# Keys and queries laid out in row halves, and one step of maxima behind the mix of every tile

## The chip, the cores and the metric

One core of a Trainium2 chip runs the whole program. The metric is device time in microseconds (us), from the launch to the end on that core; the number given for a kernel is the median of several runs.

## The reference

Two blocks, each a cross attention and a mixture of experts, on x of shape (32, 56, 256): 32 batches of 56 tokens, 256 features. The attention is the part that the change touches:

```python
q_big  = einsum('bshk,hkq->bshq', layernorm(x) @ Wq.T, w_kc_q)      # 16 heads, 192 wide; layer 0 applies rope
kv     = rope(ctx)                                                    # ctx: (32, 1500, 64)
q_r    = einsum('bshq,hqr->bhsr', q_big, W_qr)
k_r    = einsum('bld,hdr->bhlr', kv, W_kr)
attn   = softmax(einsum('bhsr,bhlr->bhsl', q_r, k_r))                 # over 1500 keys
ctx_c  = einsum('bhsl,bld->bhsd', attn, kv)
x      = x + (ctx_c through w_kc_kv) @ Wo.T
```

After it come, in layer 0, a router over 16 experts of which 4 are taken and a shared expert, and in layer 1 a dense feed-forward with eight low-rank adapters, two of them for each token.

## The kernel before, in words

The weights are merged once at the start (W_kr into the queries' side), so that every head's query is 64 wide and meets the same 64-wide keys. Then each layer runs a loop over 4 groups of 8 batches; a group has 448 tokens, and a batch has 16 heads x 56 tokens = 896 query columns.

A group begins with the queries of all heads (`qwide`, `query`). To keep precision, a value is split in a part that the fast matmul form holds exactly and a rest: `kparts` has the keys' high part in rows 0 to 63 and their low part in rows 64 to 127; `qhigh` holds the high part of the queries twice, once in each half of the rows; `qlow` holds the low part in rows 0 to 63 and, in row 64, the shift of the softmax (minus the maximum). `kones` has the high keys again and a row of ones.

Then comes the attention loop over the batches j, and in it over 12 tiles t of 125 keys:

- `score` (L863, L866): four matmuls, two for each half of the 896 columns, into one of two double banks (`wide`). ScalarE takes the exponential into `prob` (L1098, four buffers).
- `mix` of the tile before (L880): prob x values, the two halves of the columns into partitions 0 to 63 and 64 to 127 of one bank.
- the sums of `prob`: GpSimd adds tiles 0 to 9 (L1211), VectorE tiles 10 and 11 (L1345), and then merges the two (L1351).
- `smax` (L841): matmuls of 128 query rows with 500 keys for the maxima of the next batch, seven rows x three column blocks = 21 a batch. VectorE reduces each to one column (L1324). They turn over the last three of four `single` banks; `SMAX_PACE` puts three of them behind the scores of tiles 2 to 8 and none at tiles 0, 1, 9, 10 and 11.
- `maxneg`, `maxT`: the maxima are joined, transposed and moved by a DMA into the shift row.
- `norm` and `share`: the sums over the partitions (L887), their reciprocal in two halves (L1370, at tiles 1 and 9) and the product with the mixed values (L1375, at tile 11).
- in layer 0 the rope of batch j + 2 (L1255 and L1262 on VectorE at tile 10, L1186 and L1187 on GpSimd) and the transposes of the keys of batch j + 1 (L806, with a copy on ScalarE, L1065, and a subtraction on VectorE, L1292) at tile 0; a DMA stores keys and values. Layer 1 fetches them (L721, L722, L729).

`schedule` writes this order out as one list of steps. Every engine walks the whole list and takes what is its own, strictly in this order, and waits on semaphores. `Regions` counts the uses of each bank: `room` makes TensorE wait until the bank's last content is drained, and what stands behind the waiting matmul in TensorE's list waits too. SP's queue, which issues all DMAs, walks the same list.

## Time and profile before

| what | value |
|---|---|
| median of 3 runs | 3490.61 us (3485.57 to 3497.17) |
| the profiled execution | 3502.88 us, its span 3501.1 us |
| TensorE (PE) matmuls busy | 3137.0 us, 90% |
| VectorE (DVE) busy | 2264.2 us, 65% |
| GpSimd (POOL) busy | 1689.7 us, 48% |
| ScalarE (ACT) busy | 1349.1 us, 39% |
| TensorE clock granted, mean | 0.938 |
| a group of layer 0, of layer 1 | some 454 us, some 388 us |

Matmuls are pipelined and their ends are modelled, so the durations of TensorE's records overlap: its real prices are the distances between the starts of blocks. The granted clock is 1.0 at 2.4 GHz and 0.5 at 1.2 GHz. An fp32 matmul is written as two records; one on split values (fp32r) is one record. "Idle before" a row names what ended the wait.

### The profile page before, as it was taken

What the parts mean: (1) busy time and instruction counts of PE and PEld (TensorE: products, weight loads), DVE (VectorE), ACT (ScalarE), POOL (GpSimd) and SP (SyncE); (2) the same over time, 40 slices, a digit from 0 to 9 for tenths busy, and PEclk for the clock granted to TensorE, in tenths of its full rate; (3) what the DMA queues carried; (4) which work ended last, traced back from release to release, by engine and by line L of the source; (5) the groups of instructions that cost most, each with busy time, mean ns of one, the idle gap of its engine ahead of it and who ended that gap; (6) DMA issues with size and microseconds to landing.
All of it is one profiled execution on the core that took longest, in us unless ns stands there. A gap on an engine that the chain in (4) does not pass through costs nothing. (4 is left out here: it accounts for less than half of the span.)

```text
span 3501.1 us, 38073 instructions
## 1 busy us (share of the span) xinstructions
PE 3137.0 (90%) x12936; PEld 1862.8 (53%) x12936; DVE 2264.2 (65%) x3034; ACT 1349.1 (39%) x1939; POOL 1689.7 (48%) x984
## 2 busy tenths in 40 slices
PE   7699978999789998899988699879998799779997
PEld 6455456555465554655547455455545455454545
DVE  3578756788567885578856467546755477555755
ACT  3235533354342553425434244333433344333442
POOL 0467624676236762367733266315642366215641
PEclk9899989999899999899999799989998899899998
DMA  7411013111131110221102211111110211111110
GB/s 258 132 39 54 32 52 96 53 40 45 36 99 48 54 49 28 81 74 42 50 35 59 93 54 40 50 54 58 53 50 6 77 53 42 47 57 55 54 53 6
DMA packets 95735, 206.20 MB, mean 59 GB/s; under 512 B 9967, under 2 KB 58783, under 8 KB 94134
## 3 DMA queue, kind: packets, MB, share of 16 engines
q1 hardware_dynamic: 95542, 203.61, 17.9%
q8 instruction: 123, 2.02, 0.2%
q14 instruction: 70, 0.57, 0.1%
HBM read 153.44 MB, written 49.91 MB: 58 GB/s over the span
## 5 line engine op out<-in xcount | busy, mean ns | idle before, releaser
L1211 POOL TENSOR_TENSOR sum_pool<-sum_pool,prob 125x896 f32<-125x896 f32 x472 | 996.6, 2111 | 232.9 <-ACT prob L1098 229.3
L1098 ACT ACTIVATE prob<-wide 125x896 f32<-125x896 f32 x768 | 704.8, 918 | 949.1 <-PE wide L866 945.1
L1324 DVE TENSOR_REDUCE maxpart<-single 128x1 f32<-128x500 f32 x1344 | 823.8, 668 | 282.6 <-PE single L841 282.1
L880 PE MATMUL single<-prob,kv 125*64 125x448 f32 x3072 | 752.1, 568 | 0.8
L863 PE MATMUL wide<-qhigh,kparts 128*125 128x448 f32 x1536 | 523.4, 422 | 10.2 <-DMA kones<-keys_merged 10.2
L863 PEld LDWEIGHTS wide<-qhigh,kparts 128*125 128x125 f32 x1536 | 231.3, 189 | 504.8 <-issue 503.4
L866 PE MATMUL wide<-qlow,kones 65*125 65x448 f32 x1536 | 445.6, 372 | 0.0
L841 PE MATMUL single<-kparts,qhigh 128*128 128x500 f32 x1344 | 406.4, 409 | 17.0 <-DVE kparts L1292 5.9
L1211 POOL TENSOR_TENSOR sum_pool<-prob 125x896 f32<-125x896 f32 x64 | 134.8, 2105 | 392.5 <-ACT prob L1098 392.5
L866 PEld LDWEIGHTS wide<-qlow,kones 65*125 65x125 f32 x1536 | 292.2, 190 | 29.8
L841 PEld LDWEIGHTS single<-kparts,qhigh 128*128 128x128 f32 x1344 | 257.5, 193 | 80.6 <-issue 26.1
L880 PEld LDWEIGHTS single<-prob,kv 125*64 125x64 f32 x3072 | 152.5, 135 | 256.1 <-issue 247.9
L1164 POOL TENSOR_TENSOR wexp_low<-wexp_low_values,wexp_high 128x768 fp32r<-128x768 f32 x68 | 128.6, 1894 | 243.5 <-ACT wexp_high L1035 243.5
L1370 DVE RECIPROCAL recip<-total 128x224 f32<-128x224 f32 x112 | 173.4, 1548 | 111.9 <-ACT total L1111 111.9
L1159 POOL TENSOR_TENSOR w_low<-w_low_values,w_high 128x384 fp32r<-128x384 f32 (+1 forms) x128 | 112.1, 879 | 186.8 <-ACT w_high L1023 186.8
L777 PE MATMUL wide<-x_high,w_high 128*96 128x448 f32 (+1 forms) x344 | 144.5, 420 | 64.3 <-POOL w_low L1159 64.2
L1196 POOL TENSOR_TENSOR sum_pool<-prob 96x448 f32<-96x448 f32 x128 | 152.0, 1206 | 61.1 <-DVE prob L1313 61.1
L1345 DVE TENSOR_TENSOR sum_dve<-prob 125x896 f32<-125x896 f32 x64 | 86.1, 1345 | 142.8 <-ACT prob L1098 142.8
L1218 POOL TENSOR_TENSOR hsum<-hid 128x448 f32<-128x448 f32 (+1 forms) x24 | 27.5, 1147 | 254.8 <-DVE hid L1483 254.8
L1186 POOL TENSOR_TENSOR rope_s<-raw,sink 125x384 f32<-125x384 f32 x32 | 37.0, 1156 | 198.7 <-POOLq L684 119.1
L778 PE MATMUL wide<-x_high,w_low 128*96 128x448 f32 (+1 forms) x344 | 131.3, 382 | 0.0
L779 PE MATMUL wide<-x_low,w_high 128*96 128x448 f32 (+1 forms) x344 | 131.0, 381 | 0.0
(272 smaller groups left out, 4414.1 us busy)
## 6 DMA issues: line engine op xcount, KB each, us to landing
wexp_low_values<-in_experts SPq DMA_DIRECT2D x68, 384.0 KB, 3.1
keys_merged<-kparts SPq DMA_DIRECT2D x32, 750.0 KB, 4.8
kparts<-keys_merged SPq DMA_DIRECT2D x32, 750.0 KB, 4.6
raw<-in_ctx SPq DMA_DIRECT2D x33, 375.0 KB
w_low_values<-w_merged SPq DMA_DIRECT2D x64, 192.0 KB, 2.4
values_merged<-kv SPq DMA_DIRECT2D x32, 375.0 KB
kv<-values_merged SPq DMA_DIRECT2D x32, 375.0 KB
kones<-keys_merged SPq DMA_DIRECT2D x96, 125.0 KB, 2.6
```

Of the source, the lines that this page charges most:

```text
L777: pe.matmul(dst, w_hi, x_hi, start=start, stop=False)
L778: pe.matmul(dst, w_lo, x_hi, start=False, stop=False)
L779: return pe.matmul(dst, w_hi, x_lo, start=False, stop=stop)
L841: pe.matmul(acc[:, 0:LB], qhigh[:, j, t * 128:(t + 1) * 128], kparts[:, kdst(j), b * LB:(b + 1) * LB], start=True, stop=True).then_inc(*R. ...
L863: pe.matmul(acc[0:LP, half, 0:HQ], kparts[:, kdst(j), cols], qhigh[:, j, q], start=True, stop=False)
L866: mm = pe.matmul(acc[0:LP, half, 0:HQ], kones[:, cols], qlow[:, j, q], start=False, stop=True)
L880: mm = pe.matmul(mix_acc[64 * half:64 * half + DC, 0:HQ], kv[:, j % 3, t, :], prob[:, (j * LT + t) % NPROB, half * HQ:(half + 1) * HQ], st ...
L1098: nc.scalar.activation(prob[:, n_ % NPROB, :].rearrange("p (a b) -> p a b", a=2), acc[0:LP, :, 0:HQ], ACT.Exp)\
L1196: nc.gpsimd.tensor_tensor(qr[:, h % 2, half, :], qa[:, h % 2, half, :], qb[:, h % 2, 1 - half, :], ALU.add)\
L1211: nc.gpsimd.tensor_tensor(dst, first_in, prob[:, n_ % NPROB, :], ALU.add).then_inc(s["pool_sum"], 1)
L1324: V.tensor_reduce(maxpart[:, j % 2, t, b:b + 1], acc[:, 0:LB], AX.X, ALU.max).then_inc(*R.signal_drained(kind, *key))
L1370: V.reciprocal(recip[:, cols], sums[:, cols])\
```

## The change

The 64-wide products are laid out in halves of the rows. `qhigh` and `qlow` hold heads 0 to 7 in rows 0 to 63 and heads 8 to 15 in rows 64 to 127, half as many columns as before; the keys, high and low, stand in both halves. A `score` is then four pairs of 64-row matmuls: high x high, low x high, high x low, and a row of ones with the shift. The second copy of the keys comes by DMA (in layer 0 from the first half, in layer 1 each half is fetched). `kones` and its copies go.

A step of maxima is a pair too: 112 query rows of either half with the same 500 keys, into the pair of banks 4 and 5 (`PAIR`), reduced by one instruction over 2 x 500 columns. A batch has 12 such steps instead of 21 matmuls; there is one at each tile, behind the mix, four tiles ahead of its use. `Regions` makes the pair exclude its two banks.

Queries are made in pairs of heads (column halves in layer 0, merged weights of two heads in layer 1). Keys' transposes come one a tile at tiles 5, 6 and 7, two batches ahead, all on bank 3; the rope moves to tile 3. For batches 0 to 6 the reciprocal of the sums is taken on 112 x 8 values: two small DMAs, one reciprocal, a store to DRAM and two broadcast loads replace the two of 128x224.

```diff
-NMAX = NQ // 128
+TQ = HQ // 4
+NMAX = 8
+NPAIR = H // 2
+PAIR = 6
-SMAX_PACE = (0, 0, 3, 3, 3, 3, 3, 3, 3, 0, 0, 0)
-EARLY_MAX = 1
-HSLOTS = (4, 6)
+EARLY_MAX = 4
+HSLOTS = (4, 8)
...
+    def maximum(j, n):
+        add("smax", j, n % 4, n // 4, region=PAIR)
...
         for t in range(LT):
+            ahead = (j + 1, t + EARLY_MAX) if t + EARLY_MAX < LT else (j + 2, t + EARLY_MAX - LT)
             add("score", j, t, region=t % 2)
-            for _ in range(SMAX_PACE[t]):
-                if ahead:
-                    row, c = ahead.pop(0)
-                    add("smax", j + 1, row, c, region=turn())
             if j + 1 < BG and t == 8:
                 add("maxneg", j + 1)
             if last is not None:
                 add("mix", *last)
                 if last[1] == LT - 1:
                     add("context", last[0])
+            if ahead[0] < BG:
+                maximum(*ahead)
             last = (j, t)
-            if layer == 0 and 0 < j < BG - 1 and t == 0:
-                keys(j + 1)
             if t == 1 and j:
-                add("norm", j - 1, region=turn())
-            if t in SHARE_AT and j:
-                add("share", j - 1, SHARE_AT.index(t))
+                add("norm", j - 1, region=3)
+            if layer == 0 and t in (5, 6, 7) and j + 2 < BG:
+                keys(j + 2, t - 5)
+            if t == 3 and j:
+                add("spread", j - 1)
+            if t == SHARE_AT[2] and j:
+                add("share", j - 1, 2)
             if j + 1 < BG and t == 9:
-                add("maxT", j + 1, region=turn())
-            if layer == 0 and t == 10 and j + 2 < BG:
+                add("maxT", j + 1, region=3)
+            if layer == 0 and t == 3 and j + 2 < BG:
                 add("rope", j + 2)
...
+        meets = {PAIR: (PAIR, 4, 5), 4: (4, PAIR), 5: (5, PAIR)}
...
                     elif kind == "smax":
-                        pe.matmul(acc[:, 0:LB], qhigh[:, j, t * 128:(t + 1) * 128], kparts[:, kdst(j), b * LB:(b + 1) * LB],
-                                  start=True, stop=True).then_inc(*R.signal_filled(kind, *key))
+                        for half in range(2):
+                            mm = pe.matmul(acc[0:TQ, half, 0:LB], qhigh[rows_of(half), j, t * TQ:(t + 1) * TQ],
+                                           kparts[rows_of(half), j % 3, 0, b * LB:(b + 1) * LB], start=True, stop=True)
+                        mm.then_inc(*R.signal_filled(kind, *key))
...
                     elif kind == "score":
+                        for i, (part, q) in enumerate(((0, qhigh), (1, qhigh), (0, qlow))):
+                            for half in range(2):
+                                pe.matmul(acc[0:LP, half, 0:HQ], kparts[rows_of(half), j % 3, part, cols], q[rows_of(half), j, :],
+                                          start=(i == 0), stop=False)
+                        if t == 0:
+                            pe.wait_ge(s["shift_loaded"], 32 * (j + 1))
                         for half in range(2):
-                            pe.matmul(acc[0:LP, half, 0:HQ], kparts[:, kdst(j), cols], qhigh[:, j, q], start=True, stop=False)
-                        for half in range(2):
-                            mm = pe.matmul(acc[0:LP, half, 0:HQ], kones[:, cols], qlow[:, j, q], start=False, stop=True)
+                            mm = pe.matmul(acc[0:LP, half, 0:HQ], c["ones_row"][rows_of(half), 0:LP], shift[rows_of(half), j % 2, :],
+                                           start=False, stop=True)
...
-                        V.tensor_reduce(maxpart[:, j % 2, t, b:b + 1], acc[:, 0:LB], AX.X, ALU.max).then_inc(*R.signal_drained(kind, *key))
+                        V.tensor_reduce(maxpart[:, j % 2, t:NMAX:4, b], acc[0:TQ, :, 0:LB], AX.X, ALU.max).then_inc(*R.signal_drained(kind, *key))
```

SP's part of it, in the order of the list:

```diff
                     if kind == "fetch":
-                        sp.dma_start(kparts[:, kdst(j), :].bitcast(F32), scratch["keys"][BG * g + j]).then_inc(s[f"keys_moved_{j % 3}"], 16)
+                        for half in range(2):
+                            sp.dma_start(kparts[rows_of(half), j % 3, :, :].rearrange("p a l -> p (a l)").bitcast(F32),
+                                         scratch["keys"][BG * g + j]).then_inc(s[f"keys_moved_{j % 3}"], 16)
...
+                    if kind == "keyT":
+                        sp.wait_ge(*R.drained("keyT", j, b))
+                        sp.dma_start(kparts[DC:2 * DC, j % 3, :, cols].bitcast(F32), kparts[0:DC, j % 3, :, cols].bitcast(F32))\
+                            .then_inc(s[f"keys_twice_{b}"], 16)
...
+                    if kind == "norm" and key[0] < BG - 1:
+                        sp.wait_ge(*R.drained("norm", j))
+                        for half in range(2):
+                            sp.dma_start(packed[half * ZP:(half + 1) * ZP, :], total[64 * half:64 * half + 1, :]).then_inc(s["sums_packed"], 16)
+                    if kind == "spread":
+                        sp.wait_ge(s["packed_recip"], j + 1)
+                        sp.dma_start(scratch["zrec"][j].rearrange("(p c) -> p c", c=ZC), packed_recip[:]).then_inc(s["recip_stored"], 16)
+                        sp.wait_ge(s["recip_stored"], 16 * (j + 1))
+                        if j:
+                            sp.wait_ge(s["ctx_ready"], j)
+                        for half in range(2):
+                            sp.dma_start(recip[64 * half:64 * half + 64, :],
+                                         scratch["zrec"][j:j + 1, half * HQ:(half + 1) * HQ].broadcast_to([64, HQ])).then_inc(s["recip_spread"], 16)
```

## Rows read from the trace of the kernel before

**Rows 1.** The page, parts 1 and 5: engines, and the sums on GpSimd.

```profile
PE 3137.0 (90%) x12936; PEld 1862.8 (53%) x12936; DVE 2264.2 (65%) x3034; ACT 1349.1 (39%) x1939; POOL 1689.7 (48%) x984
...
L1211 POOL TENSOR_TENSOR sum_pool<-sum_pool,prob 125x896 f32<-125x896 f32 x472 | 996.6, 2111 | 232.9 <-ACT prob L1098 229.3
```

**Rows 2.** Windows: start:end, length, busy us by engine, granted clock, DMA share, GB/s.

```profile
665.30:896.70 231.40, 231.40 (x1018) 118.99 (x1017) 176.14 (x221) 116.36 (x156) 156.24 (x77) 0.99 0.11 39
...
1953.00:1997.70 44.70, 32.74 (x127) 26.97 (x128) 23.84 (x41) 14.35 (x35) 11.69 (x16) 0.81 0.38 115
1997.70:2221.90 224.20, 224.20 (x944) 112.70 (x945) 144.39 (x190) 96.69 (x117) 141.07 (x67) 0.99 0.14 42
```

**Rows 3.** Timeline in a loop of layer 0: start, us, engine, line.

```profile
318.68 0.68 PE L863 MATMUL wide<-qhigh,kparts 128*125 128x448 f32 x2
...
319.60 0.85 PE L841 MATMUL single<-kparts,qhigh 128*128 128x500 f32 x3
...
320.03 1.85 DVE L1324 TENSOR_REDUCE maxpart<-single 128x1 f32<-128x500 f32 x3 [0.75 <-PE single L841]
320.38 0.97 PE L880 MATMUL single<-prob,kv 125*64 125x448 f32 x4
...
321.28 0.67 PE L863 MATMUL wide<-qhigh,kparts 128*125 128x448 f32 x2
...
322.29 0.97 PE L880 MATMUL single<-prob,kv 125*64 125x448 f32 x4
...
327.23 0.62 DVE L1375 TENSOR_TENSOR ctx_n<-ctx_raw,recip 128x448 f32<-128x448 f32 x1
```

**Rows 4.** The chain that ended last, in order of time: four fp32 records, 128 columns wide.

```profile
3480.67 1.50 PE single L990 x4
```

**Rows 5.** Groups on VectorE in a loop of layer 0 (665.3 to 896.7): busy us, mean ns.

```profile
L1324 DVE TENSOR_REDUCE maxpart<-single 128x1 f32<-128x500 f32 x144 | 88.4, 669 | 31.9 <-PE single L841 31.8
L1370 DVE RECIPROCAL recip<-total 128x224 f32<-128x224 f32 x14 | 21.7, 1548 | 7.7 <-ACT total L1111 7.7
L1255 DVE TENSOR_TENSOR rope_c<-raw,cosk 125x768 f32<-125x768 f32 x6 | 15.4, 2559 | 0.0
...
L1351 DVE TENSOR_TENSOR sum_dve<-sum_dve,sum_pool 125x896 f32<-125x896 f32 x7 | 10.4, 1485 | 0.2
L1262 DVE TENSOR_TENSOR kv<-rope_c,rope_s 125x768 f32<-125x768 f32 x6 | 7.5, 1255 | 0.2
```

**Rows 6.** Groups ahead of that loop (572.5 to 665.3), queries of layer 0.

```profile
L1196 POOL TENSOR_TENSOR sum_pool<-prob 96x448 f32<-96x448 f32 x32 | 38.0, 1206 | 15.3 <-DVE prob L1313 15.3
...
L1312 DVE TENSOR_TENSOR prob<-wide,cosq 96x896 f32<-96x896 f32 x16 | 17.4, 1086 | 12.5 <-PE wide L779 11.3 <-POOL sum_pool L1196 1.2
...
L1159 POOL TENSOR_TENSOR w_low<-w_low_values,w_high 128x384 fp32r<-128x384 f32 x16 | 16.0, 1003 | 6.2 <-ACT w_high L1023 6.2
```

**Rows 7.** Groups on VectorE in a loop of layer 1 (1997.7 to 2221.9).

```profile
L1351 DVE TENSOR_TENSOR sum_dve<-sum_dve,sum_pool 125x896 f32<-125x896 f32 x7 | 7.6, 1092 | 0.2
```

**Rows 8.** Timeline at the start of a group of layer 0, GpSimd idle.

```profile
575.64 0.96 DVE L1255 TENSOR_TENSOR rope_c<-raw,cosk 125x768 f32<-125x768 f32 x1 [5.14 <-issue]
```

**Rows 9.** DMA issues of the whole run: count, KB each, median us to landing.

```profile
kparts<-keys_merged SPq DMA_DIRECT2D x32, 750.0 KB, 4.6
...
kones<-keys_merged SPq DMA_DIRECT2D x96, 125.0 KB, 2.6
```

**Rows 10.** Timeline from the last maxima of batch 0 to the loop.

```profile
657.18 0.17 DVE L1331 TENSOR_REDUCE maxneg<-maxpart 128x7 f32<-128x21 f32 x1
...
665.31 0.92 ACT L1098 ACTIVATE prob<-wide 125x896 f32<-125x896 f32 x1 [2.44 <-PE wide L866]
```

**Rows 11.** Timeline of TensorE among the queries of layer 1.

```profile
1971.09 0.44 PE L777 MATMUL wide<-x_high,w_high 128*128 128x448 f32 x1 [4.11 <-POOL w_low L1159]
...
1973.01 0.57 PE L778 MATMUL single<-x_high,w_low 128*128 128x448 f32 x1
1973.38 0.57 PE L779 MATMUL single<-x_low,w_high 128*128 128x448 f32 x1
```

More of the change, by code:

```diff
@@ L47 @@
 MT = -(-HID // 128)
+ZP, ZC = 56, 8
 SHARE_AT = (1, 9, 11)
[L50 removed]
 RT = NT // 112
@@ L133, in schedule @@
+    last_maxima(0)
     add("maxneg", 0)
[L134 removed]
     if layer == 0:
[L137 to L138 removed]
+        keys(1, 0)
+    add("maxT", 0, region=3)
+    if layer == 0:
+        keys(1, 1)
+        keys(1, 2)
+    for n in range(EARLY_MAX):
+        maximum(1, n)
     last = None
[L140 to L141 removed]
     for j in range(BG):
[L144 removed]
```

299 lines of the change are left out of this document (146 added, 153 removed).

## The prediction

> **What bounds the kernel now.** I read the page first: TensorE is busy 90% of the span, VectorE 65%, GpSimd 48% [rows 1]. By stage, the attention loops (eight batches of twelve tiles) take 231.4 us in a group of layer 0 and 224.2 in one of layer 1, and in both TensorE is never idle at a granted clock of 0.99 [rows 2]. Eight such loops are 4 x (231.4 + 224.2) = 1822 us, half the time. VectorE is busy 176 of 231 us in layer 0: second in line. The stretch ahead of the loop, where queries are made, is 44.7 us in layer 1, and TensorE is not full there (busy 32.7, granted 0.81) [rows 2]; in layer 0 it is longer and holds the maxneg and exp of [rows 10] at its end.
>
> Inside a loop the timeline of TensorE gives the price of each step [rows 3]: scores (four matmuls) to mix 1.01 us (321.28 to 322.29), mix to scores 0.90 (320.38 to 321.28), so a tile without maxima is 1.91. With three maxima it is 2.60 (318.68 to 321.28): 0.23 for one. Check: 96 x 1.91 + 144 x 0.23 = 216.5; the other 15 of the 231.4 are seven norms (about a mix each), seven maxT and six runs of key transposes.
>
> **The scores: nothing.** Four matmuls of 128 and 65 rows become four pairs of 64-row halves (three products and the shift). No row of before shows row halves. The nearest is the mix, two 64-column halves: four records in 0.90 us [rows 3], where four records of the same 448 columns on the full array take 1.50 [rows 4]. So halves of columns do run at the same time, and I take halves of rows to do so: four units before, four after. Bounds: no overlap costs four units a tile; imperfect overlap is the 0.15 us by which 0.90 exceeds half of 1.50, over two passes 0.075 a pair.
>
> **The maxima on TensorE: a gain.** 21 matmuls a batch become 12 pairs. In the loops 144 x 0.23 = 33.1 us become 80 x 0.23 = 18.4 (16 of the 96 pairs of a group stand ahead of the loop): -14.7 a loop, -118 over eight. Transposes, norm and maxT now stand between maxima and scores, in halves of columns amid halves of rows, and the transposes in three runs instead of one. A change of form costs about 0.1 us (1.01 for a score block against 4 x 0.23 x 448/500 = 0.82, two changes a tile): +18 (0 to 37).
>
> **The maxima on VectorE: no gain, and one buffer.** A reduction of 128x500 takes 0.669 us and a PSUM read of 896 columns 1.086 [rows 5, 6]: 1.05 ns a column, so the new 1000 columns take 1.19. Twelve of these are 14.3 us a batch, the old 21 were 14.0. What changes is the room. Before, three banks turn and the pace leaves tiles 0, 1, 9, 10 and 11 free of maxima. After, each tile has one step of maxima, and all use the one pair of banks. TensorE waits at a step until the reduction of the step before is over, and behind the waiting matmul stand the next scores, the exponentials and everything else. Count from the start of a step of maxima: the reduction begins after 0.1 (load) + 0.43 (319.60 to 320.03 [rows 3]) and ends at 1.72; other VectorE work W and the next reduction end at 2.91 + W; 0.06 later TensorE may fill the pair for the step after that, and it wants to at 2 x (1.91 + 0.23) = 4.28. So it stalls for W - 1.3, where that is positive. Maxima back to back cost 1.72 + 0.06 = 1.78 each.
>
> - Batch boundary, between the maxima of tiles 11 and 0: ctx_n 0.62, the last sum and the merge of sums, both 896 columns from SBUF at 1.09 [rows 3, 7], are 2.8, a stall of 1.5. Six boundaries a loop, eight loops: +72 (with the mean of layer 0, 1.49 [rows 5], for both, W is 3.6 there: +91).
> - The rope of layer 0, now at tile 3, where GpSimd adds sums in 2.11 us out of 2.14 [rows 1, 5]. Before it began at the end of GpSimd's run. rope_c takes 0.96 us with GpSimd idle [rows 8] and 2.56 on average in the loop, the final add of the same size 1.26 [rows 5], 0.96 if alone. With the small reciprocal (some 0.18, as maxneg [rows 10]): W = 0.18 + 2.56 + 1.26 = 4.0, a stall of 2.7, 24 times: +65. Bounds: GpSimd never in the way, W = 2.1, 24 x 0.8 = 19; both operations held for a whole 2.11, W = 0.18 + 2 x 3.07 = 6.3, 24 x 5.0 = 120.
> - The keys' subtractions (64x500, taken at the 0.67 of a reduction of 500 columns) come one a tile: below 1.3, nothing.
>
> On this the trace shows rope_c at 0.96 alone and 2.56 in the loop [rows 5, 8]. The Trainium skill ("SBUF — State Buffer", on who interferes with whom) says that GpSimd and a VectorE operation with two SBUF inputs take an exclusive lock for the whole instruction. By that rule the second operation could wait too, and the sum would have the 120 in place of the 65, 55 us more; the trace agrees for one operation and leaves open who wins the next turn.
>
> **Reciprocals.** Two of 1.55 us a batch [rows 5] go; they have no place of their own in the stalls above, so this is what keeps those from being worse. In their place come two small moves, one reciprocal, a store and two broadcasts. The sums are copied about 2.0 us after the maxima of tile 1 (norm as a mix 0.9, a copy of half the columns of an exponential 0.5, signals; an estimate), and VectorE comes to the reciprocal at 4.28 + 1.72 = 6.0: cover of 4 us for moves of which the small ones take 2.6 [rows 9]. In layer 1 the fetch of keys and values is issued at tile 0 ahead of them, and it grows from 750 + 375 to 2 x 750 + 375 KB because each row half gets its copy. At 4.6 us for 750 KB [rows 9] that is 11.5 us, where the reciprocal is wanted 9.6 after the maxima of tile 0 (3 x 2.14 + 1.5 + 1.72): at most 1.9 late, W = 2.1, a stall of 0.8. Bounds 0 and 20 x 0.8 = 16; I take +5. SP waits in its own queue for the store of the reciprocals, with the next context load and the key copies behind it; these are wanted tiles later. In layer 0 a 256 KB copy of the keys into the other rows leaves 2.4 us after the maxima of tile 5 and is wanted at tile 8, 4.9 later; it should land between the 2.6 of 125 KB and the 4.6 of 750 [rows 9]. The shift leaves at tile 9 behind the key store of tile 7 (375 + 750 KB) and is wanted some 4 us later. Both nothing; where that cover fails, up to 3 us x 24 = 72.
>
> **Ahead of the loops.** Layer 0: the keys' three transposes share one bank, so TensorE waits twice for a copy and a subtraction of 500 columns, 0.67 each by the reduction, and signals: +3.2. Queries take half the passes, but three maxima in a row now cost 1.78 each, and GpSimd needs 2 x 1.21 + 1.00 = 3.4 us a head [rows 6], where TensorE's part now is 12 x 0.20 + 1.5 = 3.9 [rows 3, 4]: nothing (-8 to +4). At the end a full row of maxima stays after the last query (+2.6), and the first maxima of batch 1 wait for keys transposed, split and copied across (about 5.4 us after maxneg, then four at 1.78 and the scores, 12.8 in all) where today exp follows maxneg by 8.1 us (657.18 to 665.31) [rows 10]: +4.7. Together +10.5 a group, +42 (20 to 70). Layer 1: 48 matmuls of 0.2 us and a 4.11 us wait for weights [rows 11] go, but sixteen maxima at 1.78 (at half clock, where one takes 0.2 more, 1.98) are 28 to 32 us of a chain with little beside it. With 9.6 us of queries (part of them at the lower clock), two waits and the scores, the 44.7 us become 44 to 49: +6 for four groups (-4 to +16). Setup copies less: -5.
>
> **Sum.** -118 + 18 + 72 + 65 + 5 + 42 + 6 - 5 = +85. The profiled run took 3502.88 us (span 3501.1 and 1.8 around it); the median of the runs shown is 3490.61, 0.35% below. Against the median the sum gives 3490.6 + 85 = 3575, with its own range of 3515 to 3640 (down by the rope near its low bound, up by the rope near its high one or the clock, below).
>
> **A price that the sum leaves out.** After 4.1 us of idleness the matmuls soon stood 0.37 us apart (1973.01 to 1973.38) and not 0.20, the lower of the two clocks [rows 11]; if a stall of 2.7 us brings three such microseconds, it adds 1.5 us, 24 x 1.5 = 36. It is in the own range.
>
> **Rivals.**
> - *Vector work stays out of the way* (faster). Place: the two clusters in the loop. If TensorE never waits for the pair, the 137 us of stalls go: 3438, and with shorter stretches ahead of the loops 3400. For it: VectorE has 24 us of work in a batch of 28. Against: the order of its queue puts 2.8 and 4.0 us between two reductions that hold the only buffer. It decides where the 72 stalls cost under (137 - 85) / 72 = 0.7 us on average. Chance 0.26.
> - *Halves overlap only in part.* 0.075 us a pair, four pairs a tile and 768 tiles (+230), less the 0.20 x 768 = 154 of change of form that the block already holds, and 0.075 x 768 = 58 for maxima: +134, 3709. Chance 0.12. In numbers of a page: the Trainium skill ("TensorE: Matmul & The Clock Gate", Part 3, measured speedup) has four row tiles at 3.07 times one; an estimate from it is 1.3 units a pair, 0.06 us over, (4 + 1) x 768 x 0.06 = 230, and 3805. No run here shows row tiles yet.
> - *Halves do not overlap.* 4 x 0.205 x 768 = +630, maxima 0.23 x 768 = +177, stalls 75 less (tiles 1.04 us longer, 72 places): 4307. For it, only that nothing in the trace shows row halves; against it, the mix. Chance 0.07.
> - *It nets out*: the rope and the stretches ahead of the loops at their low bounds, -118 + 18 + 72 + 19 + 20 - 4 - 5 = +2, 3492. Chance 0.08.
>
> **Chances and range.** The forecast has 0.47. A measurement here can tell about 0.3% (10 us) from no change. Slower: 0.47 + 0.12 + 0.07 = 0.66; same 0.08; faster 0.26. The range runs from 3405, into the faster case, to 3690; left out are the bottom of that case, most of the part overlap and no overlap, about 0.2.
>
> **What would show it.** Right: score block near 1.0 us and a tile at 2.14 in quiet steps; TensorE idle before the maxima of tiles 1 and 5, released by the reduction, 1.5 and 2.7 us; reductions of 1.19; a loop of layer 0 near 245 us and of layer 1 near 220. Wrong: no idle time at those maxima (faster), a score block of 1.3 or more (part overlap) or 1.8 (none), or idle time ahead of the reciprocal released by a move.

## The result, and the profile after

Before 3488.1 us (3482.3 to 3497.2), after 3787.9 us (3783.9 to 3792.3), medians of four runs each. The ratio on record is 1.0846, 95% interval 1.0825 to 1.0867 (the two medians alone give 1.0860). The change costs 300 us. The forecast was 3575 with a range from 3405 to 3690: the sign was right, the size short by 213 us, and the time lies 98 us above the range. The profiled execution has a span of 3783.0 us, 282 more than before.

The exponentials on ScalarE cut the span (the time from the first instruction to the last) into stages: a loop is counted from the start of its first exponential to the start of its last. All numbers are us; the last column is the last experiment, in which all mends stand together:

| stretch | before | after | difference | forecast | last experiment |
|---|---|---|---|---|---|
| start to the first loop | 209.3 | 233.4 | +24 | | 221.3 |
| four loops of layer 0 | 922.7 | 1079.4 | +157 | +51 | 906.6 |
| between them | 668.5 | 716.0 | +48 | | 682.4 |
| from layer 0 to layer 1 | 197.2 | 205.7 | +9 | | 194.7 |
| four loops of layer 1 | 896.4 | 911.7 | +15 | -9 | 846.7 |
| between them | 491.6 | 520.0 | +28 | | 481.5 |
| the end | 115.4 | 116.6 | +1 | | 116.7 |
| all outside the loops | 1682.0 | 1791.7 | +110 | +43 | 1696.6 |

The forecast's column is its sum split by layer: for a layer (-118 + 18 + 72) / 2 = -14, with 65 for the rope in layer 0 and 5 for the reciprocals in layer 1.

The page of after, part 1 and the rows of part 5 that answer to [rows 1, 5] (us busy, mean ns; idle time before, and who ended it):

```profile
PE 3122.5 (83%) x16008; PEld 1727.9 (46%) x16008; DVE 2096.5 (55%) x2343; ACT 1261.1 (33%) x1747; POOL 1654.5 (44%) x952
...
L1317 DVE TENSOR_REDUCE maxpart<-pair 112x2 f32<-112x1000 f32 x768 | 920.4, 1198 | 739.8 <-PE pair L840 739.8
...
L840 PE MATMUL pair<-kparts,qhigh 64*112 64x500 f32 x1536 | 403.4, 522 | 286.5 <-DVE maxpart L1317 264.1
```

TensorE is busy as long as before (3122 for 3137 us) in a longer span, and VectorE does less (2097 for 2264 us). 264 us of TensorE's idleness stand in front of the pair of banks. The windows of a loop of layer 0, of the stretch ahead of a loop of layer 1, and of that loop, as in [rows 2]:

```profile
741.60:1012.00 270.40, 242.42 (x1414) 113.04 (x1414) 157.76 (x150) 107.25 (x135) 156.59 (x77) 0.93 0.24 57
2180.00:2234.60 54.60, 28.97 (x92) 19.10 (x94) 24.20 (x25) 8.28 (x19) 5.75 (x8) 0.63 0.55 125
2234.60:2465.00 230.40, 214.22 (x1344) 100.51 (x1343) 122.19 (x121) 97.34 (x117) 140.59 (x67) 0.98 0.21 50
```

Before, the granted clock was 0.99 in both loops and 0.81 in the stretch ahead of one [rows 2]; now it is 0.93, 0.98 and 0.63. So idleness is one part of the cost and a lower clock the other.

**The rope in layer 0.** Timeline of a batch, from the reciprocal of tile 3 on (start, us, engine; in brackets the idle time ahead):

```profile
353.03 0.19 DVE L1350 RECIPROCAL packed_recip<-packed 112x8 f32<-112x8 f32 x1
353.14 1.49 DVE L1248 TENSOR_TENSOR rope_c<-raw,cosk 125x768 f32<-125x768 f32 x1
...
353.96 2.62 POOL L1204 TENSOR_TENSOR sums<-sums,prob 125x896 f32<-125x896 f32 x1
...
354.67 2.73 DVE L1255 TENSOR_TENSOR kv<-rope_c,rope_s 125x768 f32<-125x768 f32 x1
...
357.32 1.19 DVE L1317 TENSOR_REDUCE maxpart<-pair 112x2 f32<-112x1000 f32 x1
...
358.56 0.55 PE L840 MATMUL pair<-kparts,qhigh 64*112 64x500 f32 x2 [2.81 <-DVE maxpart L1317]
```

Between the end of the reduction ahead (353.11, from 351.91) and the next one at 357.32 lie 4.2 us of other work; TensorE waits 2.81 at the maxima of tile 5. The forecast had 4.0 and 2.7. What it left beside the sum stands in the windows behind that wait:

```profile
355.70:358.50 2.80, 0.05 (x2) 0.00 (x0) 2.80 (x2) 0.10 (x1) 2.66 (x2) 1.00 0.26 82
358.50:362.90 4.40, 4.34 (x19) 2.14 (x19) 1.88 (x3) 1.50 (x2) 0.83 (x1) 0.61 0.30 98
362.90:367.00 4.10, 4.10 (x28) 2.18 (x28) 2.52 (x3) 1.65 (x3) 3.12 (x2) 1.00 0.35 77
```

After 2.8 us without a matmul TensorE works the next 4.4 us at a granted clock of 0.61, mostly the lower level, 1.2 GHz.

**The shift in layer 0.** SP's queue and TensorE at the turn of a batch:

```profile
331.38 0.44 SPq L714 DMA_DIRECT2D values_merged<-kv  x1
332.07 0.62 SPq L718 DMA_DIRECT2D keys_merged<-kparts  x1
334.44 2.13 SPq L746 DMA_DIRECT2D shift<-maxrow  x2
...
341.08 0.47 PE L866 MATMUL wide<-shift,ones_row 64*125 64x448 f32 x2 [1.91 <-DMA shift<-maxrow]
```

The shift is issued 2.4 us behind the store of 750 KB and is there 6.6 us after its issue. The list of TensorE's waits has this 24 times, 44.0 us in the run; before, the shift is not in it.

**The sums in layer 1.** The fetch, the small move of the sums, the reciprocal and TensorE:

```profile
2726.30 1.19 SPq L700 DMA_DIRECT2D kparts<-keys_merged  x2
...
2731.39 1.73 SPq L730 DMA_DIRECT2D packed<-total  x2
...
2739.42 0.20 DVE L1350 RECIPROCAL packed_recip<-packed 112x8 f32<-112x8 f32 x1 [2.96 <-DMA packed<-total]
...
2740.74 0.48 PE L840 MATMUL pair<-kparts,qhigh 64*112 64x500 f32 x2 [1.68 <-DVE maxpart L1317]
```

Two moves of 1.8 KB take 8.0 us, with 1875 KB of keys and values issued 5.1 us ahead of them; that the one is the cause of the other is shown below, where the fetch stands behind the sums. They land 13.1 us after the fetch; the forecast had 11.5, wanted after 9.6.

**Ahead of the loops.** The wait for the keys at the start of a group of layer 1, and three of the ten steps of maxima just ahead of its loop, each 2.06 us behind the last:

```profile
2194.71 0.48 PE L840 MATMUL pair<-kparts,qhigh 64*112 64x500 f32 x2 [4.15 <-DMA kparts<-keys_merged]
...
2217.00 0.76 PE L840 MATMUL pair<-kparts,qhigh 64*112 64x500 f32 x2 [1.30 <-DVE maxpart L1317]
...
2219.06 0.76 PE L840 MATMUL pair<-kparts,qhigh 64*112 64x500 f32 x2 [1.30 <-DVE maxpart L1317]
...
2221.12 0.76 PE L840 MATMUL pair<-kparts,qhigh 64*112 64x500 f32 x2 [1.30 <-DVE maxpart L1317]
```

TensorE and VectorE take turns on one pair of banks: of the 2.06 us the reduction takes 1.20, and TensorE stands still for 1.30. The granted clock of the whole stretch is the 0.63 above.

### The profile page after: what moved, and what is told of

Read it like the earlier page. It is cut to its first block and busy times, and to the rows that moved or that the text cites. A ratio compares the mean times of both kernels' runs of the same rounds, so it can differ in the third digit from the quotient of the medians.

```text
span 3783.0 us, 43017 instructions
## 1 busy us (share of the span) xinstructions
PE 3122.5 (83%) x16008; PEld 1727.9 (46%) x16008; DVE 2096.5 (55%) x2343; ACT 1261.1 (33%) x1747; POOL 1654.5 (44%) x952
## 5 line engine op out<-in xcount | busy, mean ns | idle before, releaser
L1317 DVE TENSOR_REDUCE maxpart<-pair 112x2 f32<-112x1000 f32 x768 | 920.4, 1198 | 739.8 <-PE pair L840 739.8
L1204 POOL TENSOR_TENSOR sums<-sums,prob 125x896 f32<-125x896 f32 x472 | 1016.5, 2154 | 305.1 <-ACT prob L1091 259.5
L840 PE MATMUL pair<-kparts,qhigh 64*112 64x500 f32 x1536 | 403.4, 522 | 286.5 <-DVE maxpart L1317 264.1
L861 PE MATMUL wide<-qhigh,kparts 64*125 64x448 f32 x3072 | 491.0, 399 | 0.0
L861 PEld LDWEIGHTS wide<-qhigh,kparts 64*125 64x125 f32 x3072 | 278.4, 193 | 160.2 <-issue 130.4
L866 PE MATMUL wide<-shift,ones_row 64*125 64x448 f32 x1536 | 296.7, 382 | 44.0 <-DMA shift<-maxrow 44.0
L861 PE MATMUL wide<-qlow,kparts 64*125 64x448 f32 x1536 | 295.5, 380 | 0.0
L866 PEld LDWEIGHTS wide<-shift,ones_row 64*125 64x125 f32 x1536 | 151.8, 193 | 67.8 <-DMA shift<-maxrow 53.1
L1189 POOL TENSOR_TENSOR sums<-prob 96x448 f32<-96x448 f32 x128 | 143.6, 1143 | 72.8 <-issue 56.3
L861 PEld LDWEIGHTS wide<-qlow,kparts 64*125 64x125 f32 x1536 | 151.4, 193 | 15.2
```

The source lines that it names most:

```text
L840: mm = pe.matmul(acc[0:TQ, half, 0:LB], qhigh[rows_of(half), j, t * TQ:(t + 1) * TQ], kparts[rows_of(half), j % 3, 0, b * LB:(b + 1) * LB] ...
L861: pe.matmul(acc[0:LP, half, 0:HQ], kparts[rows_of(half), j % 3, part, cols], q[rows_of(half), j, :], start=(i == 0), stop=False)
L866: mm = pe.matmul(acc[0:LP, half, 0:HQ], c["ones_row"][rows_of(half), 0:LP], shift[rows_of(half), j % 2, :], start=False, stop=True)
L1189: nc.gpsimd.tensor_tensor(qr[:, h % 4, half, :], qa[:, h % 2, half, :], qb[:, h % 2, 1 - half, :], ALU.add)\
L1204: nc.gpsimd.tensor_tensor(dst, first_in, prob[:, n_ % NPROB, :], ALU.add).then_inc(s["pool_sum"], 1)
L1317: V.tensor_reduce(maxpart[:, j % 2, t:NMAX:4, b], acc[0:TQ, :, 0:LB], AX.X, ALU.max).then_inc(*R.signal_drained(kind, *key))
```

## The experiments

Each is the changed kernel with one edit, unless it says otherwise. Times are medians; the ratio is to the kernel before, run beside it (3491 to 3494 us), with its 95% interval.

### The place of the maxima

```diff
+            if ahead[0] < BG:
+                maximum(*ahead)
             if j + 1 < BG and t == 8:
                 add("maxneg", j + 1)
             if last is not None:
                 add("mix", *last)
...
-            if ahead[0] < BG:
-                maximum(*ahead)
```

> One part of the change is undone: each step of maxima stands behind the scores of its tile and ahead of the mix, as before. Main theory (the time went into clumps of vector work around the one pair of banks, not into the place): the reduction of a step starts 0.9 us earlier and so does the next, the waits stay what they are, so the time stays at 3788 within 15 us, and TensorE still idles 2.5 to 3 us ahead of the maxima of tile 5. Rival (the place behind the mix is the cause): the time falls by 150 us or more, towards 3490 to 3640. A third theory: with the mix behind the maxima, the mix waits with them, the probabilities are freed later and the exponentials fall behind: slower by 20 us or more.

Measured: 3855.9 us, 1.1055 (1.1023 to 1.1088), 68 us slower than the change. The first two theories fall; the third had the sign and a size that fits (20 us or more), but the loss is in layer 1 alone. The loops of layer 0 stay (1083 for 1079 us); those of layer 1 take 969 for 912, and 5 us come outside. A batch of layer 1:

```profile
2771.94 0.20 DVE L1350 RECIPROCAL packed_recip<-packed 112x8 f32<-112x8 f32 x1 [4.93 <-DMA packed<-total]
...
2773.26 0.76 PE L840 MATMUL pair<-kparts,qhigh 64*112 64x500 f32 x2 [3.45 <-DVE maxpart L1317]
...
2777.54 0.92 ACT L1091 ACTIVATE prob<-wide 125x896 f32<-125x896 f32 x1 [6.77 <-PE wide L866]
```

The sums land 12.9 us after the fetch, as they did (13.1), but VectorE and TensorE reach it sooner: 4.93 and 3.45 us of idleness for 2.96 and 1.68. And ahead of the waiting maxima TensorE has done only the scores of the tile; the mix waits behind them. So the new place helps the changed kernel; it is not what made it slow.

The same question on the kernel before, whose three maxima of a tile were put behind the mix:

```diff
-            for _ in range(SMAX_PACE[t]):
-                if ahead:
-                    row, c = ahead.pop(0)
-                    add("smax", j + 1, row, c, region=turn())
-            if j + 1 < BG and t == 8:
-                add("maxneg", j + 1)
             if last is not None:
...
+            for _ in range(SMAX_PACE[t]):
+                if ahead:
+                    row, c = ahead.pop(0)
+                    add("smax", j + 1, row, c, region=turn())
+            if j + 1 < BG and t == 8:
+                add("maxneg", j + 1)
```

> The kernel before with nothing changed but the place of its maxima: the three of a tile stand behind the mix and not behind the scores (maxneg of tile 8 behind them). With three banks in turn and 2 us of maxima on VectorE in a tile, neither place makes TensorE wait: the time stays at 3490 within 10 us (theory: the place alone is worth nothing). Rival (the place matters by itself: the exponential of a tile starts at the same moment but its mix has 0.7 us less cover, or the last maxima of tile 8 come 0.9 us later and with them the shift): 20 us or more slower.

Measured: 3504.0 us for 3494.3, 1.0030 (1.0015 to 1.0045): a difference of 10 us, at the edge of what was called the same. The place alone costs some 10 us, and a row of its list of TensorE's waits (us in total, times, longest) says where: the transposed maxima wait for their last reduction 56 times, where before they did so 8 times, 13.3 us in all. The tile of it, tile 9, takes 2.5 for 2.2 us.

```profile
PE single L846 <- DVE maxneg L1331: 21.8, 56, 1.9
```

### The lower clock behind the stall

```diff
             if ahead[0] < BG:
+                if layer == 0 and t == 5 and j + 2 < BG:
+                    add("fill", j)
                 maximum(*ahead)
...
+                    if kind == "fill":
+                        for _ in range(14):
+                            pe.matmul(region[3][0:LP, 0:HQ], kparts[0:DC, key[0] % 3, 0, 0:LP], qhigh[0:DC, key[0], :],
+                                      start=True, stop=True)
+                        continue
```

> In layer 0, ahead of the maxima of tile 5, TensorE gets 14 extra matmuls of 64 rows (125 x 448, 0.19 us each, 2.7 us) into a bank that nobody reads; the wait for the reduction stays where it is. Main theory (a stall of 2.8 us is followed by some microseconds at the lower clock, which cost as much again): the idle time ahead of those maxima goes, the maxima run at the same moment, the tiles behind them keep the higher clock, and tile 5 to 7 give back about 2.5 us in each of 24 batches: 3788 - 60 = 3730 (3700 to 3750); the loop of layer 0 goes from 270 to about 255 us, and its granted clock from 0.93 to 0.96 or more. Rival (the time between the maxima and the next exponentials is vector or scalar work that comes late, not the clock): no gain, 3788 or up to 30 us slower.

Measured: 3746.5 us, 1.0733 (1.0705 to 1.0760), 41 less with more work. A loop of layer 0:

```profile
728.20:985.10 256.90, 245.70 (x1496) 121.47 (x1498) 157.38 (x149) 106.97 (x134) 156.95 (x77) 0.98 0.25 60
```

256.9 for 270 us, granted clock 0.98 for 0.93. From the exponential of tile 5 to that of tile 6 it is 5.8 us where it was 7.1: what remains is a quiet tile, the transposes and the stall (2.13 + 0.74 + 2.9). The rest was the clock: 53 us over the four loops, some 2.2 a stall. (The loops are read from the profiled run, which at 3733.3 us was 13 us below the median; hence 53 here and 41 in the medians.)

### The rope in two tiles

```diff
-            if layer == 0 and t == 3 and j + 2 < BG:
-                add("rope", j + 2)
+            if layer == 0 and t == 2 and j + 2 < BG:
+                add("ropec", j + 2)
+            if layer == 0 and t == 4 and j + 2 < BG:
+                add("rope", j + 2)
...
```

> In layer 0 the first product of the rope on VectorE goes to tile 2 and its final add to tile 4, one tile step apart from each other, where both stood at tile 3. Nothing else is changed. Main theory (4.2 us of other vector work between two reductions that hold the one pair of banks cause the stall of 2.8 us, and the stall causes the low clock): W becomes about 1.5 to 2.7 at each of the two places, the excess of tiles 5 and 6 over 2.13 falls from 5.9 us a batch to 2 or less, 24 x 4 = 96 us less: 3692 (3670 to 3720), a loop of layer 0 of about 246 us. Rival (the bank is not the limit but the total vector work, or the clock is low for another reason): the excess moves to other tiles and the time stays within 25 us of 3788.

Measured: 3664.6 us, 1.0495 (1.0461 to 1.0530): 123 less, 5 us beyond the range that was expected. The four loops of layer 0 take 957 us for 1079, tile 5 to 6 takes 3.04 for 7.1. VectorE and the sum of GpSimd in one batch:

```profile
367.81 1.49 DVE L1250 TENSOR_TENSOR rope_c<-raw,cosk 125x768 f32<-125x768 f32 x1
369.23 1.19 DVE L1321 TENSOR_REDUCE maxpart<-pair 112x2 f32<-112x1000 f32 x1
...
371.41 3.61 POOL L1206 TENSOR_TENSOR sums<-sums,prob 125x896 f32<-125x896 f32 x1
...
372.11 0.95 DVE L1259 TENSOR_TENSOR kv<-rope_c,rope_s 125x768 f32<-125x768 f32 x1
```

The same two operations take 2.4 us where back to back they took 4.2, and neither holds a reduction for more than 1.5. The final add takes 0.95 again (mean of the loop 948 ns for 2725), as long as beside an idle GpSimd [rows 8], though GpSimd is not idle: its sum began at 371.41, 0.70 ahead of the add, and this time it is the sum that takes longer, 3.61 us for 2.10. In the changed kernel the sum beside the final add had begun 0.71 ahead of it as well, and there the add took 2.73. So who pays is not settled by which of the two records begins first.

### The store behind the shift

```diff
-                    if kind == "keyT" and key[1] == 2:
+                    if (kind == "keyT" and key[1] == 2 and key[0] < 2) or (layer == 0 and kind == "maxT" and 2 <= key[0] + 1 < BG):
+                        if kind == "maxT":
+                            sp.wait_ge(*R.drained("maxT", key[0]))
+                            ...
+                        j = key[0] + (kind == "maxT")
...
```

> In layer 0 the store of keys and values of batch j + 2 stands in the DMA queue behind the move of the shift (tile 9) and not ahead of it (tile 7). Main theory (the move of the shift lands late because 1125 KB of stores are in front of it): the wait of TensorE for the shift, 11.0 us in a loop of six batches, goes; part of it returns as the 1.5 us at the maxima of tile 0 that the late start covered. 24 x (1.9 + some 1.5 of low clock behind it - 1.5) = 46: 3742 (3715 to 3765). Rival (the shift waits for something else, its own small packets or the transposed maxima): the wait stays at 11 us in a loop and the time within 15 us of 3788.

Measured: 3744.9 us, 1.0739 (1.0706 to 1.0773), 43 less. In the loops no wait for the shift is left (the four of layer 0 take 1037 us for 1079), and the stall at the batch boundary that it had covered appears; the waits of a loop of layer 0 are now

```profile
PE pair L845 <- DVE maxpart L1322: 23.8, 12, 2.9
```

where there were 17.0 us in 6, and 11.0 for the shift.

### The fetch behind the sums

```diff
-            if layer == 1 and t == 1 and 2 < j + 2 < BG:
-                add("fetch", j + 2)
...
             if t == 1 and j:
                 add("norm", j - 1, region=3)
+            if layer == 1 and t == 1 and 2 < j + 2 < BG:
+                add("fetch", j + 2)
```

> In layer 1 the fetch of keys and values two batches ahead (2 x 750 + 375 KB) stands in the DMA queue behind the small move of the sums, some 5 us later. Main theory (the move of the sums takes 8 us because the fetch is in front of it, the reciprocal waits for it on VectorE, the next reduction behind the reciprocal, and TensorE behind the reduction): VectorE's wait for the packed sums, 21.4 us in a loop of layer 1, goes to under 3; tiles 5 and 6 of batches 1 to 5 lose their excess of 1.5 to 4 us, some 2.2 on average: 20 x 2.2 = 44 us less, 3744 (3725 to 3765). Rival (the keys then land after tile 8, where their first maxima are due, and the wait goes there; or the move of the sums is slow by itself): within 15 us of 3788.

Measured: 3740.0 us, 1.0712 (1.0687 to 1.0736), 48 less. The keys come five microseconds later, and nothing waits for them. The loop of layer 1 and its waits of VectorE and TensorE:

```profile
2238.10:2454.90 216.80, 210.02 (x1340) 99.24 (x1340) 121.65 (x119) 96.43 (x116) 140.81 (x67) 1.00 0.22 53
```
```profile
DVE packed_recip L1350 <- DMA packed<-total: 5.7, 1, 5.7
```
```profile
PE pair L840 <- DVE maxpart L1317: 6.8, 6, 1.2
```

The packed sums cost 5.7 us in place of 21.4, once, in the last batch, which has no maxima. What TensorE still waits is the batch boundary, 1.1 us at each of six; behind these short waits the clock does not fall (1.00 over the loop).

### The merge behind the maxima of tile 0

```diff
                 if last[1] == LT - 1:
                     add("context", last[0])
             if ahead[0] < BG:
                 maximum(*ahead)
+            if last is not None and last[1] == LT - 1:
+                add("merge", last[0])
...
-            if t == 1 and j:
+            if t == 2 and j:
                 add("norm", j - 1, region=3)
...
-            if t == 3 and j:
+            if t == 5 and j:
                 add("spread", j - 1)
...
```

> VectorE merges the sums behind the maxima of tile 0 and not ahead of them, the product with the ones comes at tile 2 and the reciprocal at tile 5. Main theory (what counts is the vector work between two reductions that use the one pair of banks: 2.8 us at the batch boundary, of which 1.7 stay): the stall of 1.2 to 1.4 at tile 0 or 1 goes in layer 1 (24 x 1.3 = 31 less); in layer 0 it was mostly hidden by the wait for the shift, so little is gained there, and the rope at tile 3 loses only the reciprocal (0.2 x 24 = 5). The reciprocal is two tiles later, so most of the wait for the packed sums goes too (up to 44): sum -70, 3718 (3690 to 3745). Rival (the boundary's excess is the product with the ones and the shift alone): only the packed wait goes, 3740 or more.

Measured: 3713.1 us, 1.0640 (1.0615 to 1.0665), 75 less, as expected. In a loop of layer 1 no wait for the pair is left at all, and it takes 210.8 us:

```profile
2233.60:2444.40 210.80, 210.33 (x1340) 99.52 (x1342) 120.33 (x119) 96.46 (x116) 145.00 (x67) 0.99 0.23 55
```

The edit moves three things at once, so what the boundary alone was worth is read against the run above, which has no wait for the sums either: 217 to 211, 6 us a loop for 6.8 us of waits. The rival falls.

### A shorter reduction

```diff
-V.tensor_reduce(maxpart[:, j % 2, t:NMAX:4, b], acc[0:TQ, :, 0:LB], AX.X, ALU.max)
+V.tensor_reduce(maxpart[:, j % 2, t:NMAX:4, b], acc[0:TQ, :, 0:LB // 2], AX.X, ALU.max)
```

> The reduction reads the first 250 of each 500 columns of the maxima, so the shift is the maximum over half of the keys; the matmuls, banks and order are unchanged. It tests the formula of the stall, stall = W - 1.3 with a reduction of 1.19 us. With 0.67 us the reduction appears twice in it, so it becomes W - 2.3: at the rope in layer 0 the stall of 2.8 us goes to 1.8, at the batch boundary 1.4 goes to 0.4, and each of 16 maxima in a row ahead of a loop costs 1.26 for 1.78. Main theory: 24 x 1.5 (1.0 and half a microsecond of low clock) + 24 x 1.0 + 20 x 0.5 + 8 x 8 = 134 less: 3654 (3620 to 3690). Rival (TensorE's own work or the transfers set the pace, the reduction being in their shadow): within 25 us of 3788.

Measured: 3700.0 us, 1.0587 (1.0557 to 1.0618): 88 less, not 134, and 10 us outside the expected range. The formula holds where vector work alone is the cause: the tile at the boundary of layer 1 takes 3.46 for 4.51 (1.05 less, as expected), and 58 us go outside the loops. At the rope the wait is 2.3 us on average for 2.8, half of what was expected, since rope_c still ends when GpSimd's sum does; tile 5 to 6 takes 6.0 for 7.1. It fails where the cause is a transfer. VectorE comes to the packed sums sooner and waits longer, 28.3 us in a loop of layer 1 for 21.4:

```profile
DVE packed_recip L1350 <- DMA packed<-total: 28.3, 6, 5.7
```

There tile 5 to 6 grows from 4.0 to 4.7 us (mean of batches 1 to 5). The loops of layer 1 gain nothing (912 us), those of layer 0 give 21 us.

### Ahead of the loops

```diff
     def last_maxima(j):
         for c in range(3):
-            add("smax", j, 3, c, region=PAIR)
+            add("smax", j, 3, c, region=(PAIR, 0, 1)[c])
...
         for c in range(3):
-            keys(0, c)
+            add("keyT", 0, c, region=3 + c)
...
     for n in range(EARLY_MAX):
-        maximum(1, n)
+        add("smax", 1, n % 4, n // 4, region=(PAIR, 0, 1)[n % 3])
```

> Ahead of the loops only: the last three maxima of batch 0 and the first four of batch 1 take turns over three double banks (the pair and the two of the scores), and the first three key transposes of layer 0 have a bank each. Main theory (seven maxima in a row cost 1.78 us each, 2.06 at the lower clock, because TensorE and VectorE alternate on one pair; with three they cost a reduction of 1.2): 7 x 0.7 = 5 us less in each of 8 groups, and 4 x 3 for the transposes: 3788 - 50 = 3738 (3715 to 3755). Rival (the stretch is set by the queries, the landing of the keys or the move of the shift, with the maxima beside it): within 15 us of 3788.

Measured: 3765.8 us, 1.0787 (1.0763 to 1.0810), 22 less where 50 was expected: neither theory. Layer 1 gives back 23 us in the stretches ahead of its loops, layer 0 next to nothing. In layer 0 the transposes end 3.1 us sooner, and TensorE then waits for the weights of a head:

```profile
659.32 0.66 PE L773 MATMUL wide<-x_high,w_high 128*96 128x448 f32 x1 [4.71 <-POOL w_low L1152]
```

The time went into a wait that had lain beside the transposes. The second step spreads the nine maxima of batch 0 among the queries:

```diff
-            if n >= 7 and n % 4 == 3 and n < H:
-                for c in range(3):
-                    add("smax", 0, n // 4 - 1, c, region=PAIR)
+            if n >= 6 and n % 4 != 1 and n < H + 1:
+                add("smax", 0, (n + 2) // 4 - 2, (n + 2) % 4, region=PAIR)
...
-            add("query", p, region=p % 3)
-            if p >= 3 and p % 2:
-                for c in range(3):
-                    add("smax", 0, p // 2 - 1, c, region=PAIR)
+            add("query", p, region=(2, 3, 1)[p % 3])
+            for n in range(max(0, 2 * p - 7), max(0, 2 * p - 5)):
+                add("smax", 0, n // 3, n % 3, region=(PAIR, 0)[n % 2])
...
```

> Ahead of the loops only. Beside what the run with more banks had, the nine maxima of batch 0 that stood three in a row stand one at a head step (layer 0) or two at a query on two double banks (layer 1). Main theory (three in a row cost 5.3 to 6.2 us in which TensorE does little and falls to the lower clock; one between two heads costs its 0.2): layer 0, 3 x 4 = 12 us less a group, layer 1 some 6 less a group because the landing of the keys holds it: with the 22 us of the run with more banks, 3788 - 22 - 72 = 3694 (3675 to 3735). Rival (the head steps are paced by GpSimd and VectorE, 3.4 to 4 us each, and the maxima are in that shadow): not below 3750.

Measured: 3689.5 us, 1.0570 (1.0545 to 1.0595), 98 less together and 76 for this step. Everything outside the loops takes 1692 us for 1792 (before: 1682). The maxima had not lain in the shadow of GpSimd and VectorE.

### All of it together

The four mends for the four causes, the rope at tiles 2 and 4, the reciprocal at tile 4 in layer 0 and 5 in layer 1:

> All the mends together on the changed kernel: rope in two tiles, store behind the shift, merge of the sums behind the maxima of tile 0 with the product at tile 2, reciprocal at tile 4 or 5, more banks and maxima among the queries ahead of the loops. Main theory (the 300 us are the sum of these places): a loop of layer 0 is then 12 x 2.13 + 1.1 (product) + 3 x 0.74 (transposes) + 0.55 = 29.4 a batch, 229 us in all for 270 (4 x 41 = 164 less), a loop of layer 1 211 for 228 (4 x 17 = 68 less), ahead of the loops what the run with maxima among the queries gives (some 90): 3788 - 320 = 3468, 0.6% faster than before (3440 to 3510). Rival (when one wait goes, the next one behind it shows, the shared limit being VectorE): 3550 or more.

Measured: 3501.2 us, 1.0020 (1.0008 to 1.0033): 287 less than the change, 33 more than expected and inside the range. One wait is new:

```profile
360.10 2.77 DVE L1265 TENSOR_TENSOR kv<-rope_c,rope_s 125x768 f32<-125x768 f32 x1
...
362.80 1.19 DVE L1327 TENSOR_REDUCE maxpart<-pair 112x2 f32<-112x1000 f32 x1
363.02 0.59 PE L810 MATMUL single<-ident,kv 125*64 125x125 f32 x4 [2.07 <-DVE kv L1265]
```

With the turn of the batch shorter and the product in tile 2, VectorE meets GpSimd in another phase: the final add takes 2.77 us for 0.95, and now the transposes of tile 5 are the first to want it. So the rope went to tiles 1 and 2:

> As the run with all mends, but with the two parts of the rope at tiles 1 and 2 for 2 and 4. In that run TensorE waited 35 us in the loops of layer 0 for the rope's result (2.07 us at the transposes of tile 5, 20 times, with some lower clock behind it), because the final add, held by GpSimd, took 2.8 us directly ahead of them. Main theory: with two tiles between, this wait goes and the maxima of tiles 2 and 3 show at most a few tenths: 20 x 2.5 = 50 less, 3451 (3435 to 3475), 1.1% faster than before. Rival (the final add beside the merge and the reductions makes a stall at the maxima of tile 3 of the same size): 3490 to 3505.

Measured: 3443.7 us (3440.0 to 3453.7), 0.9854 (0.9831 to 0.9876): 344 us less than the change and 1.5% faster than before. A loop of layer 0 and one of layer 1, in the columns of [rows 2]:

```profile
675.40:902.30 226.90, 225.68 (x1412) 106.35 (x1414) 149.31 (x150) 106.98 (x134) 160.43 (x77) 0.99 0.29 71
2005.00:2216.80 211.80, 211.32 (x1340) 99.77 (x1340) 120.16 (x119) 96.48 (x116) 145.01 (x67) 0.99 0.23 54
```

TensorE is idle for 1.2 and 0.5 us of them, at a clock of 0.99, and they are 4.5 and 12.4 us shorter than before. Alone, the rope gave 123 us, the store 43, the merge with the later reciprocal 75, and the stretches ahead of the loops 98: 339 in sum. The same four together gave 287; the 52 us between are the new wait at tile 5 (8.9 us in a loop of layer 0, 36 in all) and what follows it, and moving the rope once more gave 57 back. So these four places hold the 300 us of the change and some more. That 339 and 344 agree so closely is not a proof that the parts are independent: the rope at tiles 1 and 2 was not run alone.

## Why the prediction was wrong

**What held.** The sign, and the mechanism: one pair of banks, and vector work in front of a reduction that holds it. Row halves run at the same time: in the timeline a quiet tile is 2.13 us (forecast 2.14), the records of a pair begin within 4 ns of each other in nine of ten pairs, and both rivals on overlap fall. From the 3.07 times that the Trainium skill ("TensorE: Matmul & The Clock Gate", Part 3, measured speedup) states for four row tiles, the forecast had an estimate of 0.06 us a pair; by it a quiet tile would be 2.13 + 5 x 0.06 = 2.43, and the measured 2.13 does not agree (the page's figure is for four tiles of 32 rows, here there are two of 64). The reduction is 1.20 us (1.19). The gain on TensorE is there as well: freed of stalls, the loops of layer 1 are 50 us shorter than before, where -118 / 2 + 18 / 2 = -50 was put down. In layer 0 the same is 16 and not 50: three tiles with transposes cost 3 x 0.74 = 2.2 us a batch where the three in one tile had cost 3.38 - 1.91 = 1.5, and the first batch of a loop 2.5 more (30.3 for 27.8).

**The rope's stall.** Its size was right (4.2 and 2.8 us for 4.0 and 2.7). The Trainium skill ("SBUF — State Buffer", on who interferes with whom) says that each of the two engines holds the lock for a whole instruction. The trace of the changed kernel agrees, with the turns alternating: rope_c takes 1.49, of which it spends 0.67 beside a sum of GpSimd that was under way, that engine's next sum takes 2.62 for 2.10, and the final add 2.73 behind it. So both operations waited, but not a whole 2.11 each, and the 120 us of that rule's bound did not come. Nor does the one whose record begins first always keep the other waiting (the add's 0.95 us beside the sum's 3.61, with the rope in two tiles). What failed is the step "a price that the sum leaves out": low clock behind the stall, put at 36 us and kept out of the sum. With the wait filled 41 us go from the time, 53 from the loops; with the stall itself removed, 123. It was not a possibility for the range but a term, and at 41 to 53 us a larger one.

**"Both nothing; where that cover fails, up to 3 us x 24 = 72."** The copies of the keys were covered. The move of the shift was not: it was counted as a small move that has 4 us, when its place in the queue gives it what 1125 KB ahead of it leave. It cost 43 us net: 24 waits of 1.8 us, nearly each with lower clock behind it, less the boundary's stall that it hid. The forecast named this possibility, with up to 72 us, and put it at nothing.

**"At most 1.9 late [...] I take +5."** The small moves landed 13.1 us after the fetch and not 11.5 (750 KB now land 7.8 to 9.1 us after their issue, with several under way), VectorE idled 2.96 us in the batch shown and some 3 us in each of 20, and the run without this wait is 48 us shorter. The bound of 16 was too low mostly because the stall itself was larger: TensorE's waits for the pair in a loop of layer 1 are 16.1 us, 6.8 without the late sums, so 1.9 us at each of five places and not 0.8, 37 us in all. The other 11 are an estimate of what follows it, the lower clock.

**The batch boundary** was put at +72. In layer 1 it is 25 us (36), the difference of the loops between the two experiments without a wait for the sums: 1.1 to 1.2 us at each of 24. In layer 0 it lay under the wait for the shift.

**Ahead of the loops**, +42 and +6 less 5 for the setup were 43; it was 110. The step that failed is "GpSimd needs 3.4 us a head, where TensorE's part now is 3.9: nothing". In the timeline of TensorE, counted from the first product of the rope of a group, four heads stood between 45.6 and 61.6 us before, 16.0 us; after, four took 20.4 (48.6 to 69.0, both counted from that product). Three maxima in a row put 5.1 us between two heads (690.66 to 695.73), 3.3 of them standstill, and the next queries run 0.37 us apart in place of 0.20 for 4.5 us, the lower clock. Taking them apart gave back 76 of the 110, and with more banks 98.

**Of the rivals**, none came. Part overlap would have given a number nearer to the result (3709, and 3805 by the estimate from the page) for a wrong reason: the quiet tile shows no such cost. Two errors run through the terms: a wait was priced without the lower clock behind it (the rope, the stretches ahead of the loops), and a small move with nothing or too little for the large ones ahead of it in its queue (the shift, the sums).

The point from which the forecast would have been right: with the four at their measured sizes the sum would have been 85 + 53 (clock at the rope) + 43 (shift) + 43 (sums, 48 less the 5) + 67 (stretches, 110 less 43) = 291, for 282 of span and 300 of medians. That it comes so near is in part luck, since two other terms were off and cancel: the gain of layer 0 was 34 us less than the sum holds (16 for 50), and the batch boundary was 11 less in layer 1 and some 29 less in layer 0. The last figure is an estimate: shift and boundary together are at most the 50 us between the loops of layer 0 with the rope in two tiles (957) and those of the last run (907), where the sum would hold 43 + 36.

Not tried: whether the fetch of the first keys of a layer 1 group (4.15 us of wait) could start under the feed-forward part ahead of it.

## What to carry to other kernels

Price a stall of TensorE with its aftermath: here 2.8 us of idleness were followed by 4.4 us at 0.61 of the clock, and cost 5 us. Stalls of 1.1 to 1.2 us, one a batch, were followed by none, and cost what they last. When work is packed into fewer, larger steps on one buffer, list what the draining engine does between two drains; spread that list so that no entry exceeds the slack (here 1.3 us). And look at what stands ahead of a small transfer in its queue: moves of 1.8 KB took 6.6 and 8.0 us here. The two together, with the maxima taken apart ahead of the loops, made a loss of 8.5% a gain of 1.5%.

## What the runs showed of the hardware

- Two 64-row matmuls on the two halves of the rows, in fp32r form, cost what one costs: the tile with four such pairs of scores, one pair of maxima and the mix is 2.13 us, where the tile of single matmuls was 1.91 and one matmul of maxima 0.23, 2.14 in sum.
- After 2.8 us without a matmul the granted clock was 0.61 over the next 4.4 us; 14 matmuls into a bank that nobody reads kept the loop at 0.98 and made the kernel 41 us faster. Behind stalls of 1.1 to 1.2 us, six in a loop of layer 1, the clock stayed at 1.00.
- VectorE and GpSimd, both with two SBUF operands, lengthened each other by turns: 0.95 us became 1.49 and 2.73, 2.10 became 2.62. With a sum of GpSimd begun 0.7 us ahead in both cases, the same add took 2.73 us behind another such operation of VectorE (the sum 2.62) and 0.95 behind a reduction (the sum 3.61).
- Two moves of 1.8 KB landed 8.0 us after their issue behind 1875 KB that were issued 5.1 us ahead.
